# Moving one multiply from GpSimd to VectorE, moving a second one within VectorE's queue, and splitting a product in TensorE's queue

## The reference

```
x = x + tanh(g_xattn[0]) * matmul_fp8(layernorm(x), ctx)    # activations quantised by 1x128, weights by 128x128 blocks
x = x + tanh(g_ffn[0])   * bitlinear(layernorm(x), W0)      # 8-bit activations with one global scale, ternary weights
x = x + tanh(g_xattn[1]) * attention(layernorm(x), ctx, ctx)
x = x + tanh(g_ffn[1])   * moe(layernorm(x), router, Wa, Wb) # 8 experts, top 2
```

## Time and profile before

| | |
|---|---|
| median of 3 runs | 2181.63 us (2179.07 to 2182.92) |
| profiled execution, its time | 2179.07 us |
| its span, first to last instruction | 2177.3 us |
| busy: TensorE, VectorE, ScalarE, GpSimd | 85%, 75%, 62%, 42% of the span |
| mean granted TensorE clock | 0.956 |

### The profile page before, as it was taken

The page is one execution under the profiler, slowest core; times in us unless marked ns, Lnnn a source line. Parts: engine busy times, 40 slices in busy tenths (PEclk is TensorE's granted clock), DMA queues, the critical chain, the costliest instruction groups (busy, mean ns, idle before and its releaser), DMA issues.

```text
span 2177.3 us, 26479 instructions
## 1 busy us (share of the span) xinstructions
PE 1858.2 (85%) x8716; PEld 821.6 (38%) x8716; DVE 1635.9 (75%) x2316; ACT 1357.0 (62%) x2587; POOL 921.2 (42%) x1288
## 2 busy tenths in 40 slices
PE   0277668878548999999999999999999999999997
PEld 0133223323213444444444444444444444444443
DVE  7999999998446777777777777777777777777761
ACT  5899989875145656556565656565655656565650
POOL 2887778864123333333333333333333333333320
PEclk9999888989859999999999999999999999999998
DMA  7788799977547887887888887888788787878781
GB/s 225 206 227 204 215 223 249 232 201 192 161 87 141 169 165 160 160 167 153 167 155 171 160 168 150 164 166 168 153 161 171 148 169 157 171 160 164 132 155 39
DMA packets 963531, 369.34 MB, mean 170 GB/s; under 512 B 915137, under 2 KB 931521, under 8 KB 963393
## 3 DMA queue, kind: packets, MB, share of 16 engines
q1 hardware_dynamic: 963392, 367.64, 77.8%
HBM read 105.42 MB, written 33.55 MB: 64 GB/s over the span
## 4 chain that ended last, share of the span: by engine, by line
DVE 36%; issue 20%; ACT 19%; POOL 11%; PE 7%; DMA 6%; SPq 2%; POOLq 0%; ACTq 0%; DVEq 0%
ACT slot L726 9%; DVE tiny L1236 8%; DVE tiny L977 7%; POOL tiny L582 5%; ACT arena L718 5%; POOL tiny L580 4%; DVE slot L1240 3%; ACT tiny L712 3%; PE sc L820 2%; DMA probs<-slot 2%; DMA slot<-slot 2%; DVE arena L1248 2%; DVE slot L1223 2%; ACT slot L740 2%; DVE arena L1078 1%
## 5 line engine op out<-in xcount | busy, mean ns | idle before, releaser
L1240 DVE SCALAR_TENSOR_TENSOR slot<-arena,tiny,slot 128x1024 f16<-128x1024 f32 x256 | 328.2, 1282 | 318.8 <-ACT slot L726 318.7
L726 ACT ACTIVATE slot<-arena,tiny 128x1024 f16<-128x1024 f32 x256 | 293.7, 1147 | 179.8 <-POOL tiny L582 164.9
L873 PE MATMUL sc<-arena,slot 128*128 128x512 f16 x1536 | 376.5, 386 | 33.0 <-ACT arena L718 23.2
L580 POOL TENSOR_SCALAR tiny<-tiny 128x1 f32<-128x1 f32 x256 | 99.3, 388 | 698.5 <-ACT arena L718 698.5
L1236 DVE TENSOR_REDUCE tiny<-sc 128x1 f32<-128x1024 f32 x256 | 306.0, 1205 | 13.0 <-PE sc L873 12.9
L718 ACT ACTIVATE arena<-sc,tiny,head_tab 128x1024 f32<-128x1024 f32 x256 | 308.4, 1205 | 8.6
L712 ACT ACTIVATE tiny<-tiny,head_tab 128x1 f32<-128x1 f32 x256 | 73.9, 289 | 350.6 <-DVE tiny L1236 350.6
L820 PE MATMUL sc<-probs,slot 128*128 128x512 f16 x768 | 187.5, 409 | 73.0 <-DMA slot<-slot 62.7
L873 PEld LDWEIGHTS sc<-arena,slot 128*128 128x128 f16 x1536 | 151.1, 99 | 222.5 <-ACT arena L718 32.4
L889 PE MATMUL accs<-probs,arena 128*128 128x512 f16 x512 | 194.9, 381 | 15.3 <-issue 15.2
L856 PE MATMUL accs<-wb_hi,slot 128*128 128x512 f16 x512 | 195.1, 381 | 8.6 <-DMA slot<-slot 8.6
(11 more groups left out here) (178 smaller groups left out, 3211.1 us busy)
## 6 DMA issues: line engine op xcount, KB each, us to landing
wb_hi<-in_ctx SPq DMA_DIRECT2D x36, 512.0 KB, 4.6
arena<-in_x SPq DMA_DIRECT2D x32, 512.0 KB, 3.6
x_scratch<-arena SPq DMA_DIRECT2D x32, 512.0 KB, 3.1
slot<-x_scratch SPq DMA_DIRECT2D x32, 512.0 KB, 3.8
slot<-in_ctx SPq DMA_DIRECT2D x32, 512.0 KB, 4.2
out<-arena SPq DMA_DIRECT2D x32, 512.0 KB, 3.4
slot<-in_L_ffn_weight SPq DMA_DIRECT2D x16, 512.0 KB, 3.9
slot<-in_L_ffn_Wa SPq DMA_DIRECT2D x16, 512.0 KB, 5.7
```

Source lines behind the costliest of these rows:

```text
L726: act.activation(PH[c % 2], PF[c % 2], ACT.Identity, scale=rinv[c % 2][:]).then_inc(s_ph.sem, 1)
L873: mm = pe.matmul(sc[:, c % 2, h * HALF:(h + 1) * HALF], q[i][:, c * P:(c + 1) * P], k[j][:, h * HALF:(h + 1) * HALF], start=start, stop=stop)
L1240: dve.scalar_tensor_tensor(out=PL[c % 2], in0=PF[c % 2], scalar=rinv[c % 2][:], in1=PH[c % 2], op0=ALU.mult, op1=ALU.subtract).then_inc(s_ ...
```

## The change

Three things are done. x_low moves from GpSimd to VectorE, where it stands first in iteration j (for tile j+1). c_low for the first eight context tiles moves within VectorE's iteration, from ahead of x_round_start to behind c_max. On TensorE product(j) is cut into two calls of 24 matmuls each; the first, with its waits, stands ahead of the small transposes of the iteration, the second behind them.

```diff
@@ gpsimd
-            def x_low(n):
-                pool.wait_ge(x_q.sem, x_q.at(n))
-                pool.wait_ge(x_d.sem, x_d.at(n))
-                if n >= 2:
-                    pool.wait_ge(x_turned[n % 2].sem, x_turned[n % 2].at(n // 2 - 1))
-                pool.tensor_tensor(blocks(XHL[n % 2][1]), blocks(XQ[n % 2]), spread(xdl[:, n % 4]), ALU.mult)\
-                    .then_inc(x_lo.sem, 1)
...
             for j in range(FIRST, LAST + 1):
-                if is_x(j + 1):
-                    x_low(j + 1)
@@ tensor
-            def product(j):
+            def product(j, ks):
...
-                for k in range(KB):
+                for k in ks:
...
             for j in range(FIRST, TILES):
+                if is_x(j):
+                    if j % PER_BATCH == 0:
+                        c_turned_by(pe, j + PER_BATCH - 2)
+                        c_turned_by(pe, j + PER_BATCH - 1)
+                    pe.wait_ge(x_turned[j % 2].sem, x_turned[j % 2].at(j // 2))
+                    after(pe, e_x1, j - 2)
+                    product(j, range(KB // 2))
                 if j in (-4, 4, 12):
                     c_turn_max((j + 12) // PER_BATCH)
                 if j in (-3, 5, 13):
...
                 if is_x(j):
-                    if j % PER_BATCH == 0:
-                        c_turned_by(pe, j + PER_BATCH - 2)
-                        c_turned_by(pe, j + PER_BATCH - 1)
-                    pe.wait_ge(x_turned[j % 2].sem, x_turned[j % 2].at(j // 2))
-                    after(pe, e_x1, j - 2)
-                    product(j).then_inc(mm1.sem, 1)
+                    product(j, range(KB // 2, KB)).then_inc(mm1.sem, 1)
@@ vector
+            def x_low(n):
+                dve.wait_ge(x_q.sem, x_q.at(n))
+                dve.wait_ge(x_d.sem, x_d.at(n))
+                if n >= 2:
+                    dve.wait_ge(x_turned[n % 2].sem, x_turned[n % 2].at(n // 2 - 1))
+                dve.tensor_tensor(blocks(XHL[n % 2][1]), blocks(XQ[n % 2]), spread(xdl[:, n % 4]), ALU.mult)\
+                   .then_inc(x_lo.sem, 1)
...
+                if is_x(j + 1):
+                    x_low(j + 1)
                 if is_x(j + 3):
                     x_max(j + 3)
...
-                if is_c(j + C_SPLIT) and j + C_SPLIT < PER_BATCH:
-                    c_low(j + C_SPLIT)
                 if is_x(j + 2):
                     x_round_start(j + 2)
...
                 if is_c(j + C_MAX, PER_BATCH):
                     c_max(j + C_MAX)
+                if is_c(j + C_SPLIT) and j + C_SPLIT < PER_BATCH:
+                    c_low(j + C_SPLIT)
```

## The result

| | before | after |
|---|---|---|
| median | 2181.97 us (4 runs, 2179.07 to 2182.92) | 2208.41 us (4 runs, 2207.98 to 2209.33) |
| ratio | | 1.0124, 95% interval 1.0106 to 1.0142 |
| profiled execution, its span | 2179.07, 2177.3 | 2212.75, 2211.0 |

The kernel became 26.4 us slower, with an interval of 23 to 31 us. The two profiled executions lie 33.7 us apart; a second profile of the changed kernel took 2208.1 us, 29.0 above the profile before. So 4.7 of the 33.7 is the spread between executions of one kernel.

What follows compares the result with a forecast made beforehand. VectorE was taken to bound the first phase. Loop +15.9, head +8.7, split product +11.4 and -1.8 given back make +34.2 us; added to the profiled 2179.1, 2213 us was forecast, range 2197 to 2224, slower 0.91.

Steps and rivals of the forecast that it cites:

- VectorE bounds the first phase: Loop j = -12 to 33: VectorE nearly without a gap, so work added in j = 2 to 27 lengthens the phase.
- The multiply costs 1.10 and waits 1.04 more in seven iterations: x_low on VectorE, j = 2 to 4 and 7 to 10: 1.10 + 1.04 - 1.45 = +0.69 us each, +4.8.
- The waits behind L491 come back: VectorE rows behind GpSimd's multiply shorten: L1017 gives back 1.45 or 0.33 us, L1131 1.58, L1123 and L1109 about 1.6.
- The head costs 8.7: Iterations to j = 1: late load_x(0), moved c_low and first multiplies waiting for GpSimd; +8.7 us, bounds +5 and +12.
- The stall at j = 13: c_factors on VectorE waits for c_spread, now behind 24 matmuls on TensorE; 8.0 us, not covered by anything behind.
- The stall at j = 23: L1114 on VectorE waits for small transpose L836, now behind 5.3 us of matmul on TensorE; +3.4 us.
- The end of the phase: From j = 28 on the multiplies lie in VectorE's idle time for TensorE before L1078: 0.
- the sum of 34.2: Total change: loop 15.9, head 8.7, split product 11.4, given back 1.8, added to the profiled 2179.1 us.

Runs made afterwards that it cites:

- mult_only: The kernel before with x_low alone moved from GpSimd to the front of VectorE's iteration, ahead of x_max; +18.5 us (1.0086).
- mult_behind: The kernel before with x_low alone moved to VectorE, behind x_max, and two GpSimd waits on its own finished work made explicit; +7.0 us (1.0028).
- clow_only: The kernel before with c_low alone moved behind c_max on VectorE; +4.8 us (1.0021).
- unsplit: The changed kernel with the product whole again, behind the small transposes; +18.3 us (1.0082) against the kernel before, 8.1 less than the changed kernel.
- split_only: The kernel before with only product(j) cut into two calls, the first ahead of the small transposes; +9.5 us (1.0045).
- clow_split: The changed kernel without the moved multiply: c_low moved and the product split; +15.4 us (1.0069) against the kernel before.
- stats_first: The kernel before with x_stats ahead of x_max on VectorE, two GpSimd waits made explicit, nothing moved from GpSimd; +9.9 us (1.0047).
- stats_hold: stats_first with GpSimd's x_round held until VectorE's c_round_start is done; -16.5 us by the medians against the kernel before, ratio 0.9931.

## Why the prediction was right, point by point

- *VectorE bounds the first phase, and GpSimd's time counts only where VectorE waits for it.* Shown: GpSimd was relieved of 61.7 us of multiplies and the kernel got slower; mult_only costs 18.5 us.
- *The multiply costs 1.10 and waits 1.04 more in seven iterations.* Measured +0.59 there (forecast +0.69; the wait is 0.91), +1.13 where nothing comes back (+1.10), +0.81 where L1017 had taken 0.56 (+0.77). The wait for c_round is shown by the row of 2.13 and by mult_behind, where it is gone and the row is 1.22.
- *The waits behind L491 come back.* L1017, L1021 and L1131 fall to 0.23, 0.23 and 0.69. L1109 falls from 1.82 to 0.28.
- *The head costs 8.7.* Measured 9.9 and 9.0. The parts, as lag at j = 1: 4.8 in clow_only, 6.3 in mult_only, 9.6 with both in unsplit. Its chain (load_x(0) later, then turn-taking) is the one in the rows, though I had the period at 5.7 and it is 5.6. The parts don't add up: 4.8 and 6.3 would be 11.1.
- *The stall at j = 13.* Forecast 8.0, measured 6.8 (7.0 for both waits at L1051 in the second profile). VectorE was ready 8.0 us into the iteration (7.9 forecast), and c_spread ended 14.8 us into it, not 15.9: x's transposes landed at 7.2 and the 24 matmuls took 7.3. The 0.7 left over from j = 12, which I had put at nothing (up to 1.5), made up for part of this. Undoing the split takes 8.1 us off.
- *The stall at j = 23.* This step failed. I had 3.4 us before L1114. In the profile after there is none:

```profile
472.89 0.22 PE L833 MATMUL accs<-slot 4*128 4x4 f32 x1
```

```profile
473.89 0.15 DVE L1113 TENSOR_SCALAR tiny<-accs 128x1 f32<-128x1 f32 x1
```

  The transpose has ended 0.8 us before L1113 reads it. I had kept the distance between TensorE and VectorE from before, and it did not stay: product(21), the first of three that run back to back before and after, starts 29.4 us later (445.16 against 415.81), L1113 32.4 us later (473.89 against 441.52). Without the multiply the stall exists, 1.9 us in split_only and 3.3 in clow_split; as far as these profiles show, the slower VectorE hides it. In the total the missing 3.4 is half covered, since the other terms of j = 22 to 28 make +0.5 where I had -1.2. That is luck.
- *The end of the phase.* I gave no gain to j = 29 to 32; the profiles show 1.5 and 2.1. Not traced further.
- *The size.* Against a profile of the same kernel the sum of 34.2 holds to 0.5 us for the first profile and is 5 too large for the second, and the medians say 26.4. The terms that are off are the two stalls (3.4 and 1.2 too large) and the end of the phase (1.5 to 2.1 too large), against a head that was 0.3 to 1.2 too small, the 0.7 of j = 12 and the 1.7 of j = 22 to 28; what is left is no more than the spread between executions. The forecast of 2213 lies nearer to the median of 2208.4 than the sum of 34.2 to the difference of 26.4, because I added it to a profiled execution 2.9 us below the median of its kernel. That is luck too.

Open: the parts measured alone add up to 32.8 us (18.5, 9.5 and 4.8) and the whole is 26.4. In the timed runs mult_only (1.0086) and unsplit (1.0082) don't differ, though their profiles are 3.3 us apart at j = 1. They ran on different occasions and each interval is 2.8 us wide on either side, so how much of c_low's 4.8 is hidden beside the multiply was not settled.

## What to carry to other kernels

Where VectorE rows of a small operation are far longer than their minimum, look up what GpSimd is doing at their end: the operation stands behind it, and that is time to be had. But moving the GpSimd operation to VectorE costs its whole length there, and the wait can move on to another pair, as it did in stats_first; ordering the two queues so that GpSimd's long operations fall beside VectorE's reductions, statistics and operations on PSUM took 15 to 17 us off, where moving the multiply added 18.5 and the whole change 26. In an in-order queue a short operation that another engine waits for must not stand behind a long one that itself waits for a transfer.

## What the runs showed of the hardware

- Releasing one wait can make a bigger one. With L1017's 1.45 us gone, L993 waited 1.80 in stats_first. Between L990 and L993 there is a gap of 0.03 us (L990 ends at 216.94, L993 starts at 216.97); GpSimd's x_round, whose row starts at 216.41, got its turn there: it ends at 218.92, 1.98 after L990, and L993 ends at 219.20.
- Waits of this kind make chains across both engines: in the head x_round holds c_low (2.74 us), c_low holds c_round (3.10 instead of 2.13), and c_round holds the multiply (3.13).
- Some operations of VectorE are not lengthened beside GpSimd's long ones. In stats_hold all 32 rows of L1082, which reads PSUM, last 1.28 us, and the 32 of the reduction L1017 last 1.17 to 1.21, also beside GpSimd's long operations: L1017 at 213.98 takes 1.17 while L493 runs from 213.12 to 215.02.
